# Cross-attention stage: a unit's steps in a new order, and per-engine lags behind that order

## The reference

```
h1 = adaln(x, t, norm1_w, norm1_b)
x = mha(h1, h1, attn1_wq, attn1_wk, attn1_wv, attn1_wo, attn1_bo) + x
h2 = adaln(x, t, norm2_w, norm2_b)
x = mha(h2, context, attn2_wq, attn2_wk, attn2_wv, attn2_wo, attn2_bo) + x
h3 = adaln(x, t, norm3_w, norm3_b)
x = glu_ff(h3, ff_w1, ff_b1, ff_w2, ff_b2) + x
```

## Time and profile before

| | us |
|---|---|
| three timed runs, median (lowest to highest) | 1346.85 (1343.43 to 1349.99) |
| the profiled execution, device time | 1338.89 |
| its span in the trace | 1337.1 |
| cross-attention, first exponential of unit 0 to that of unit 14 | 231.9 |
| PE busy, of the span | 1148.7 |
| DVE busy, of the span | 897.2 |

### The profile page before, as it was taken

One profiled execution on the slowest core, in us unless ns is written; L12 is line 12 of the kernel. 1 busy time (PEld: TensorE's weight loads), 2 busy tenths in 40 slices (PEclk: granted clock), 3 DMA queues, 4 the chain that ended last, 5 costly groups with the idle time before them and its releaser, 6 DMA issues.

```text
span 1337.1 us, 30602 instructions
## 1 busy us (share of the span) xinstructions
PE 1148.7 (86%) x12732; PEld 740.2 (55%) x12739; DVE 897.2 (67%) x1754; ACT 593.1 (44%) x855; POOL 640.5 (48%) x572
## 2 busy tenths in 40 slices
PE   4789999999999999999899989777777788989966
PEld 1355666566566556556566656544544555555644
DVE  5668866766676677677576685665556567675675
ACT  3345454544444444444444554333333353255655
POOL 5546765655555565665555553444234345501220
PEclk7799999999999999999999999998999989889988
DMA  7320122022112202202202221214222250000000
GB/s 257 103 56 11 39 49 49 2 49 49 26 25 49 49 2 49 49 2 49 49 2 49 49 65 39 56 38 114 61 54 42 56 166 31 0 1 17 16 1 32
DMA packets 41854, 63.52 MB, mean 48 GB/s; under 512 B 11459, under 2 KB 22383, under 8 KB 41461
## 3 DMA queue, kind: packets, MB, share of 16 engines
q1 hardware_dynamic: 40413, 60.91, 18.1%
q10 hardware_dynamic: 1304, 0.66, 0.2%
HBM read 20.63 MB, written 2.10 MB: 17 GB/s over the span
## 4 chain that ended last, share of the span: by engine, by line
PE 52%; DVE 17%; DMA 8%; issue 7%; ACT 6%; POOL 5%; SPq 3%; ACTq 1%; DVEq 0%
PE outs L742 8%; PE mixed L763 6%; PE scores L801 5%; PE scores L802 5%; DMA head_operands<-qk_pairs 4%; PE outs L824 4%; PE outs L826 3%; SPq L609 3%; PE outs L825 3%; DVE maxes L1606 3%; PE outs L876 3%; PE outs L719 3%; PE scores L860 3%; POOL exps_rest L1395 2%; PE outs L752 2%
## 5 line engine op out<-in xcount | busy, mean ns | idle before, releaser
L1395 POOL TENSOR_TENSOR exps_rest<-exps 128x1024 f16<-128x1024 f32 (+1 forms) x267 | 464.8, 1746 | 352.3 <-ACT exps L1105 351.4
L1105 ACT ACTIVATE exps<-scores 128x1024 f32<-128x1024 f32 (+1 forms) x320 | 297.8, 936 | 248.9 <-PE scores L802 248.9
L1606 DVE TENSOR_REDUCE maxes<-mixed 128x1 f32<-128x512 f32 x512 | 336.1, 684 | 61.7 <-PE mixed L763 59.1
L824 PE MATMUL outs<-values,exps 128*128 128x65 f16 (+1 forms) x2176 | 229.1, 193 | 7.3 <-POOL exps_rest L1395 6.8
L825 PE MATMUL outs<-values,exps 128*128 128x64 f16 (+1 forms) x2176 | 228.9, 192 | 0.0
L826 PE MATMUL outs<-values,exps_rest 128*128 128x65 f16 (+1 forms) x2176 | 228.7, 195 | 0.0
L801 PE MATMUL scores<-head_operands 128*128 128x512 f16 (+1 forms) x576 | 220.1, 382 | 7.8 <-DMA head_operands<-neg_max_rows 7.3
L824 PEld LDWEIGHTS outs<-values,exps 128*128 128x128 bf16 (+1 forms) x2176 | 202.0, 98 | 34.3 <-POOL exps_rest L1395 11.1
L802 PE MATMUL scores<-head_operands 128*128 128x512 f16 (+1 forms) x576 | 219.8, 382 | 0.0
L825 PEld LDWEIGHTS outs<-values,exps 128*128 128x128 bf16 (+1 forms) x2176 | 201.1, 98 | 24.0 <-issue 0.3
L763 PE MATMUL mixed<-head_operands 128*128 128x512 f16 x512 | 181.0, 389 | 26.2 <-DMA head_operands<-qk_pairs 11.6
(11 more groups left out here) (200 smaller groups left out, 1669.0 us busy)
## 6 DMA issues: line engine op xcount, KB each, us to landing
head_operands<-qk_pairs SPq DMA_DIRECT2D x128, 256.0 KB, 4.1
head_operands<-qk_pairs SPq DMA_DIRECT2D x32, 128.0 KB, 2.4
stage<-in_L_xcond_ff_w_dram SPq DMA_DIRECT2D x3, 1024.0 KB, 5.0
residual<-in_x_dram SPq DMA_DIRECT2D x4, 512.0 KB, 9.9
stage<-in_L_ffn_w_dram SPq DMA_DIRECT2D x2, 1024.0 KB, 5.2
head_operands<-in_x_dram SPq DMA_DIRECT2D x1, 2048.0 KB, 12.5
out_dram<-out_tile SPq DMA_DIRECT2D x16, 128.0 KB, 1.7
attn_outT<-in_L_xcond_attn_wq_dram SPq DMA_DIRECT2D x1, 1024.0 KB, 8.4
```

What stands on the lines that cost most here:

```text
L824: mm(o, eb[:, sl], vb[:, DH:VW], start=(kt == 0 and q == 0), stop=False, skip_group_check=True)
L1105: A(E[0:a.ks, c % RING, 0:n], SP_[c % 2][0:a.ks, 0:n], ACT.Exp, scale=SCALE).then_inc(s.exps, 1)
L1395: G.tensor_tensor(R[0:a.ks, c % RING, 0:n], e, e.bitcast(BF16).rearrange("p (n two) -> p n two", two=2)[:, :, 1], ALU.subtract).then_inc(s ...
L1606: V.tensor_reduce(mx[:, h, t, kh:kh + 1], m[:, :], AX_X, ALU.max).then_inc(s.maxed, 1)
```

## The change

`cross_slots()` and the cross-attention part of `extras()` go. A table CROSS_UNIT now lists the steps of a unit one by one. A number behind a kind is how many units ahead or behind the unit it belongs to (("q", 2, 0) is the first query half of unit g + 2); ("scores", 4) is chunk 0 of the next unit. LAGS moves kinds of steps, engine by engine, a number of places behind their place in the common list, from the start of the cross-attention on; `program(engine)` sorts by place. PE and SP keep the common order.

```diff
+CROSS_UNIT = (
+    ("normT", -1, 0), ("split", 0), ("out", -1, 0), ("out", -1, 1), ("max", 1, 0, 0), ("rest", 0),
+    ("norm", -1, 1), ("max", 1, 0, 1), ("scores", 1), ("scores", 2), ("q", 2, 0), ("lo", -1, 0),
+    ("normT", -1, 1), ("split", 2), ("hi", -1, 0), ("rest", 1), ("max", 1, 1, 0), ("hi", -1, 1), ("lo", -1, 1),
+    ("q", 2, 1), ("values", 0), ("rest", 2), ("max", 1, 1, 1), ("proj", 0), ("row", 1, 0), ("k", 2, 0),
+    ("scores", 3), ("values", 1), ("rest", 3), ("proj", 1), ("v", 1, 0), ("row", 1, 1), ("values", 2),
+    ("norm", 0, 0), ("scores", 4), ("values", 3))
+LAGS = {"DVE": {"q": 3, "max": 1, "v": 3, "rest": 2},
+        "ACT": {"row": 6, "hi": 3, "out": 2, "k": 1, "scores": 4, "q": 6},
+        "POOL": {"rest": 1, "norm": 10, "lo": 3}}
...
+    def program(self, engine):
+
+        lags = LAGS.get(engine, {})
+        at = self.cross_at
+
+        def place(i):
+            st = self.steps[i]
+            kind = st.what[0] if st.kind == "item" else st.kind
+            return i + (lags.get(kind, 0) if i >= at else 0)
+
+        return [self.steps[i] for i in sorted(range(len(self.steps)), key=place)]
...
-            for st in STEPS:
+            for st in PROGRAM["PE"]:
                 piece(st)
...
-            for st in STEPS:
+            for st in PROGRAM["ACT"]:
                 piece(st)
...
-            for st in STEPS:
+            for st in PROGRAM["POOL"]:
                 piece(st)
...
-            for st in STEPS:
+            for st in PROGRAM["DVE"]:
                 piece(st)
```

More of the change, by code:

```diff
@@ L176, in extras, with cross_unit @@
                     self.add("item", 1, v, what)
[L177 to L205, removed]
+    def cross_unit(self, a, g, first_max):
+        for kind, *at in CROSS_UNIT:
+            if kind in ("norm", "normT", "hi", "lo"):
+                v = g + at[0]
+                if v >= 0 and v // 4 % 2 == 0:
+                    self.norm(kind, (NT + TPB if v < 8 else 2 * NT) + 2 * (v % 4) + at[1])
+            elif kind == "proj":
+                ai, b, half = (1, g // 8, 0) if g // 4 % 2 else (0, 1, 1) if g < 8 else (1, 0, 1)
+                self.proj(ai, b, half, 2 * (g % 4) + at[0])
+            elif kind == "split":
+                if (g, at[0]) in CROSS_SPLITS:
+                    self.add("split", c=CROSS_SPLITS[g, at[0]])
+            elif kind in ("scores", "rest", "values"):
+                v, c = g + at[0] // a.chunks, at[0] % a.chunks
+                if 0 <= v < UNITS:
+                    self.add(kind, 1, v, c=c)
+            elif 0 <= g + at[0] < UNITS:
+                self.add("item", 1, g + at[0], first_max[at[1]][at[2]] if kind == "max" else (kind, at[1]))
     def unit(self, a, g, slots):
@@ L299, in attention @@
         self.add("scores", 1, 0, c=0)
+        self.cross_at = len(self.steps)
         self.outer_banks = (2, 3)
         for g in range(UNITS):
-            self.unit(x, g, cross_slots(n))
+            self.cross_unit(x, g, n)
+        for c in range(x.chunks):
+            if not any(s.kind == "values" and (s.ai, s.g, s.c) == (1, UNITS - 1, c) for s in self.steps):
+                self.add("values", 1, UNITS - 1, c=c)
         if LATE_OUT:
@@ L332, in build @@
     STEPS = schedule.attention()
+    PROGRAM = {engine: schedule.program(engine) for engine in ("PE", "ACT", "POOL", "DVE")}
     FF_STEPS = schedule.feed_forward()
```

## The result

The changed kernel takes **1283.4 us** (median of four runs, 1280.4 to 1288.3) against 1348.4 for the kernel before in the same comparison (1343.4 to 1350.8): a ratio of 0.953, 95% interval 0.948 to 0.957. The profiled execution took 1283.8 us, with a span of 1282.0, so the two profiles differ by 55.1 us.

The account below looks back on a forecast made before the run. It took plain and norm units to be bound by latency, neither PE nor DVE filling them. Units 0 to 13 falling from 231.9 to 173.5 us (58.4), plus 3 at the end, made 61 off the 1346.85 median: 1286, range 1266 to 1316.

Parts of the forecast that it names:

- The three waits in plain units: Units without norm tiles: PE waits 1.0 us at the key item, 1.2 and 1.5 for restacks; without them 10.65 is left.
- the row's landing: Plain units: scores wait for the DMA of the row of maxima, between 0.3 and 2.1 us, taken as 0.8.
- restack waits "near zero": Sign in the changed profile: the maxes' waits for the DMAs laying out queries and keys should be near zero.
- the wait for the row that I named as a sign: Sign in the changed profile: a new wait of scores for neg_max_rows, 0.3 to 2 us in plain units.
- Norm units: Units carrying two tiles of the next norm: DVE, busy 11.03 us, becomes the bound; with 1.5 of waits, 12.6 (11.0 to 14.0).
- The units between: Units 0, 4, 8 and 12: 10.3 us for unit 0, 12.2 each for 8 and 12, 15.2 for 4.
- The end of the stage: Unit 14 to the feed-forward: load of x issued 6 us earlier, PE arriving some 2.5 earlier; 3 us of gain taken.
- The level: Profiled run at 1338.9 us, 8 us under the timed median of 1346.85; the forecast was given against the median.
- The clock: Falls in units 4, 8, 12 and 14, 10 us by count, assumed to return; if they stay, 51 us gained instead of 61.
- (3): Rival, each unit: the row lands only behind all eight restack DMAs, so scores wait; slower, 1359 us; chance 0.05.
- (1): Rival: the row lands as late as beside a self-attention restack, 4.46 us; plain units 13.3, total about 1304; chance 0.15.
- (2): Rival, norm units: the engines' orders hold each other up, 15.2 us per unit, total about 1312; chance 0.11.

Follow-up runs that it names:

- after_again: The changed kernel run once more, unaltered, beside three follow-up kernels on one chip: 1286.6 us, ratio 0.957 to the kernel before.
- max_early: The changed kernel with the first head's two maxes back ahead of the output's two transpose groups: 1299.9 us, ratio 0.968 to the kernel before.
- x_late: The changed kernel with the 2 MB load of x held on SP until both row DMAs of unit 15 have landed: 1276.9 us, ratio 0.952.
- key_early: x_late with the key item one step further forward, ahead of the first projection, and three places late on ACT: 1328.9 us, ratio 0.988.
- key_late: The changed kernel with the key item moved behind chunk 3 of the scores, the values and the second projection: 1314.7 us, ratio 0.978.
- both_late: x_late with the 1 MB load of ffn_w1 held in the same way too: 1278.5 us, ratio 0.951 to the kernel before.
- all_three: x_late with key_early and split8_early together, rows four places late, last split moved to the middle of unit 15: 1294.8 us, ratio 0.963.
- split8_early: x_late with, on ACT alone, unit 14's first split ahead of unit 13's last exponential and rows five places late: 1277.9 us, ratio 0.952.

## Why the prediction was right

- **The three waits in plain units** were read rightly, and so was what is left: 11.70 and 11.75 us for units 6 and 8, forecast 12.0 and 12.2. The term that was too large is the row's landing, 0.8 us. It is nothing in these two units, since the row lands within the 2.3 us that PE has. I took the quiet 2.65 of the earlier trace rows as the shortest landing, which was too long (1.73 and at most 2.0 here). The restack waits "near zero" are in fact 7.6 us in all, and the wait for the row that I named as a sign stands in one plain unit only (0.40 us, in unit 5). Unit 13, which I counted as plain, took 14.42 us (13.17 in after_again); ACT's first split of unit 14 lies in it.
- **Norm units**: 12.14 to 12.88 us in units 1, 2, 9, 10 and 11, forecast 12.6, with DVE busy for 90% and 1.26 us of its waits where I allowed 1.5. But "DVE is the bound" was half of it: as max_early showed, PE's waits are not hidden there.
- **The units between** came out at 9.79 (10.3), 11.75 (12.2), 13.29 (12.2; 12.16 in after_again). Unit 4 was split otherwise than I said, since ACT's part of the split stands ahead of its first exponential: 14.83 + 12.21 for units 3 and 4, together 27.04 against 12.6 + 15.2 = 27.8. The rest beside the split took 2.71 us on POOL and cost the unit nothing, as the forecast had it. The sum of units 0 to 13 is 174.3, forecast 173.5. That they are so close is partly luck: unit 4 came out 3.0 us below its price, and units 3 and 13 2.2 and 2.4 above theirs.
- **The end of the stage** is the step that failed. I gave it 3 us of gain, and from unit 14's first exponential to the end the kernel takes 269.7 us instead of 266.9, 2.9 more. I followed the chain of the earlier trace rows through the load of x, and took an earlier load for a gain. It was wrong twice: the additions have slack, and the earlier load (7.0 us into unit 14, forecast 9.5) went ahead of the last rows, which then landed in 5.66 us. Before, it was issued 5 us behind them (1085.74 against 1080.38). So the profile gives 55.1 us where the sum says 61. The other half of my reckoning stood: with the load held, in x_late, PE reaches the feed-forward 21.5 us after unit 14's first exponential, 2.2 less than the 23.6 of before, where I gave 2.5.
- **The level**: the median fell by 65 us, not 55, because the profiled run of before lay 9.5 us under its median (1338.9 against 1348.4) and that of after on it. Part of the close hit, 1283 against 1286, is that these two errors cancel.
- **The clock**: all falls in units 4, 8 and 12 are gone, as the forecast needed; that of unit 14 is not (0.86). I had overlooked a fifth fall before, 0.91 in a norm unit:

```profile
868.13:886.82 18.69, 14.08 (x135) 9.05 (x134) 11.13 (x33) 5.96 (x14) 8.18 (x13) 0.91 0.22 47
```

  What a fall costs can be read from key_early, where equal plain units take 14.49 and 14.52 us at full clock and 16.59 at 0.90: 2.1 us. In the kernels with the restack waits back the falls came back too (0.90 and 0.88 in units 1 and 4 of key_late), and once in both_late, in unit 3 (16.83 us at 0.90 against 14.89 at 1.00 in x_late). There PE was busy for 1.34 of 3.47 us, the last 1.42 of them a wait for the restack, and the next 3 us ran at the lower level:

```profile
871.13:874.60 3.47, 1.34 (x13) 1.11 (x11) 3.05 (x9) 1.68 (x3) 2.20 (x3) 0.97 0.70 146
874.60:877.60 3.00, 3.00 (x14) 1.50 (x15) 1.45 (x5) 1.17 (x2) 0.00 (x0) 0.50 0.21 47
```

  The same place of x_late, with a wait of 1.02, kept the full clock. The page "TensorE: Matmul & The Clock Gate" of the Trainium skill (Part 1) says that idle stretches halve the clock; the fall in both_late agrees (0.50 behind the wait).
- **The rivals**: (3), a row that lands behind the restack, did not happen, and key_early speaks against its mechanism: at most 2.0 us behind four restack DMAs. (1) did not happen either, since the row landed within 2.3 us in a plain unit, nor (2), with norm units at 12.1 to 12.9 us. A price of its size exists in this kernel all the same, by the row's place on ACT (2.9 us) or by a large load (5.66).

## What to carry to other kernels

A fixed latency in a pipelined loop (here 5.2 us from the key item to the landing of the first head's restack) is paid or hidden by the work that the waiting engine has between starting it and needing it: measure that distance in us of work, for one step earlier and one later too, since here 2.1 us of work less lost 28 us, and one step further forward lost 10 us in units 0 to 13 even with the rows refitted (all_three). Lags by engine came second here, and DVE's brought nothing on the other order. When an edit lets a large load start earlier, look for a small DMA that someone waits for behind it; before counting a gain from a chain, check that shifting its first link moves its end. Here the additions ended 3.3 to 12.9 us behind the start of the next stage and the time from there on stayed within 2.5 us.

## What the hardware showed

A DMA of 2 KB took 1.73 us in x_late and 5.66 us, by the chain of the changed kernel, when 3 MB of loads had been issued on another queue up to 3.6 us before it:

```profile
1021.75 5.66 DMA head_operands<-neg_max_rows
```

It is the 2 MB load of x that makes the difference. With the 1 MB load alone ahead of it, the row took 2.24 us when that had been issued 3.6 us before (the chain of key_early), as in the changed kernel, and 1.73 at 4.4 us (x_late); issued only 1.1 us before, the 1 MB load was enough for 4.27 (split8_early).

```profile
1069.87 2.24 DMA head_operands<-neg_max_rows
```

The page "DMA: Bandwidth & Descriptors" of the Trainium skill ("Issuing engines are not separate DMA queues") says that issuing from another engine saves only the issue, since the DMA engines are shared; the trace agrees (5.66 against 1.73). Its section "Queues, rings and completion order" says that a DMA engine takes turns between queues, packet by packet; that fits a row that lands 8.1 us after the issue of a load which itself took 10.7, by the page of the changed kernel. Which packets it waited for no run shows.

```profile
head_operands<-in_x_dram SPq DMA_DIRECT2D x1, 2048.0 KB, 10.7
```
